# A transformer block with 4-bit feed-forward weights: the first half's chain first, the second half's attention among the feed-forward units

## The chip, the cores and the metric

The kernel runs on one core of a Trainium2 chip. The metric is the device time of one execution in microseconds, the median of the runs. PE is the matrix engine, DVE the vector engine, ACT the scalar engine, POOL the GpSimd engine; SP issues most of the loads.

## The reference, cut to what matters

The input x has 1024 tokens of 256 features. Six vectors of modulation come from one small product. In short:

```python
sa, ca, ga, sb, cb, gb = six 256-wide parts of silu(c) @ wmod
ga, gb = sign * maximum(abs, 0.25)
h = layernorm(x) * (1 + ca) + sa
c = h @ W_to_kv.T @ W_compress.T              # 32 features
ch = layernorm(c) * gamma + beta
q, k, v = ch @ W_q.T, ch @ W_k.T, ch @ W_v.T   # rope on q and k
o = softmax(causal(q @ k.T / sqrt(32))) @ v
z = o @ W_comp2lat.T
x = x + ga * (z @ W_to_kv + z @ W_out_res.T + b_out_res)
h = layernorm(x) * (1 + cb) + sb
gate, up = h @ Wg.T, h @ Wu.T                  # 2048 features, 4-bit weights with scales
x = x + gb * ((gelu_tanh(gate) * up) @ Wd.T)
```

## The kernel before, in words

Each engine has one list of instructions in program order, and the lists meet only in semaphores; the order written in the code is the order in which an engine runs.

The 1024 tokens are two halves of 512 (`h` 0 and 1), each of four tiles of 128. Attention is causal, so the first half has 4 key blocks and the second 8 (`blocks(h)`). Products that need accuracy are made of three matmuls on a high and a low part: ACT writes the high part (a rounded copy) and DVE or POOL the low part (value minus high part). So the probabilities exist as PH (ACT, a second exp) and PL (`probs_low`), the hidden state as H with `h_hi` and `h_lo`, the weights as WS with `split_gu`/`split_d` (ACT) and `low_gu`/`low_d` (POOL), the product of gate and up as IS with `inter_hi` (ACT) and `inter_low` (POOL, later DVE).

The feed-forward has 8 groups of 256 features. A unit is one half of a group for one half of the tokens: 16 units (0 to 15) for the first half of tokens, then 16 for the second. For unit n PE does `gate_up(n)`, 12 matmuls of 512 columns, and two units later `down(n)`, 12 matmuls of 256 columns. In between ACT does `gelu(n)`, DVE `inter_full(n)` (gelu times up), ACT `inter_hi(n)`, POOL `inter_low(n)`. `gate_up(n+1)` waits for `gelu(n)` and `inter_full(n)`, since one pair of PSUM banks serves all units except unit 1, which has banks of its own.

The weights of group G serve units 2G and 2G+1. They come as 4-bit codes: ACT takes the bytes (`take_bytes`), DVE decodes in five steps (`decode`, lines 692 to 704), ACT splits (`split_gu`, line 398, which waits for the decoded group), POOL makes the low part. Groups 0 and 1 are decoded by hand-placed calls, the others by `decode_more` after each `inter_full`, with six steps done before unit 0 (`STEPS_AT_START`).

The order now: both halves go through the norm, the latent projection and q, k, v in an interleaved way, then the second half's scores, row maxima and its exps of blocks 0 to 6 are done before `gate_up(0)`; the rest of its attention lies between units 0, 1 and 2, and `output(1)` behind `gate_up(2)`. The residual and the statistics of the second half are done by DVE after units 1 to 3.

`stay_warm` issues matmuls on a tile of zeros. The table of functions of ACT is loaded ahead of the first exp and ahead of the first gelu. All copies, casts and scalings on ACT go with either.

Of the kernel before, what the change touches and what calls it, by code (L numbers as in the profile page):

```python
# [67 lines left out]
STEPS_AT_START = 6  # L68
H0_BLOCK = 4
# [3 lines left out]
def build_block(nc, x, wmod, c_col, attn64, attn32, b_out, consts, rope, packed, scales, out):  # L73
    with ExitStack() as ctx:  # L74
# [10 lines left out]
        MODA_B, GA_B, WC_B, WO_B = 4, 5, 6, 7  # L85
# [7 lines left out]
        bout_sb = sb("bout_sb", [P, D])  # L93
# [13 lines left out]
        gab = sb("gab", [P, D])  # L107
        gb_b = sb("gb_b", [P, D])
        wsum = sb("wsum", [DLAT, D])
# [46 lines left out]
        x_in = [sem("x_in0"), sem("x_in1")]  # L156
        c_in, a64_in, a32_in, cst_in, bout_in, rope_in = sem("c_in"), sem("a64_in"), sem("a32_in"), sem("cst_in"), sem("bout_in"), sem("rope_in")
# [8 lines left out]
        wsum_ready = sem("wsum_ready")  # L166
# [4 lines left out]
        moda_done = sem("moda_done")  # L171
# [8 lines left out]
        gab_ready = sem("gab_ready")  # L180
# [20 lines left out]
        xres_ready = sem("xres_ready")  # L201
# [83 lines left out]
        def unit_banks(n):  # L285

            return (Y, Y + 1) if isinstance(n, int) and n == 1 else (GATE, UP)
# [5 lines left out]
        def _(sp):  # L293
            sp.dma_start(xres[:, 0:HT, :], x_d[:, 0:HT, :]).then_inc(x_in[0], 16)
            sp.dma_start(cst[:], consts).then_inc(cst_in, 16)
            sp.dma_start(wmod_sb[:, :, 0:2 * D], wmod_d[:, :, 0:2 * D]).then_inc(wmod_in[0], 16)
            sp.dma_start(xres[:, HT:, :], x_d[:, HT:, :]).then_inc(x_in[1], 16)
            sp.dma_start(wmod_sb[:, :, 2 * D:], wmod_d[:, :, 2 * D:]).then_inc(wmod_in[1], 16)
            sp.dma_start(rope_sb[:], rope).then_inc(rope_in, 16)
# [13 lines left out]
        def _(act):  # L313
            act.dma_start(c_sb[:], c_col).then_inc(c_in, 16)
            act.dma_start(a64[:], attn64).then_inc(a64_in, 16)
            act.dma_start(a32[:], attn32).then_inc(a32_in, 16)
            act.dma_start(bout_sb[:], b_out.unsqueeze(0).to_broadcast([P, D])).then_inc(bout_in, 16)
# [5 lines left out]
            def norm1_out(h):  # L323
                act.wait_ge(t1_done, h + 1)
                if h == 1:
                    act.wait_ge(c_done, 1)
                for k in range(KT) if h else (0,):
                    act.activation(xnT[:, k, :], bank(4 * h + k), ACT.Copy).then_inc(t1_ready, 1)

# [34 lines left out]
            def stage_h0():  # L364
# [3 lines left out]
                for e in range(2):  # L368
                    if e == 1:
                        act.wait_ge(h_full, 1)  # L370
                    act.activation(H[:, 0, 0, e, :], bank(e), ACT.Identity, bias=mods[:, M_SB + e:M_SB + e + 1],
                                   scale=mods[:, M_CB + e:M_CB + e + 1]).then_inc(h_hi, 1)

# [45 lines left out]
            norm1_out(0)  # L419
            take_bytes(0)  # L420
# [53 lines left out]
        def _(pool):  # L474
# [16 lines left out]
            def add_bias(h):  # L491

                pool.wait_ge(gab_ready, 1)
                pool.wait_ge(x1n_ready, HT * (h + 1))
# [702 lines left out]
```

## Time and profile before

| | us |
|---|---|
| median of 3 runs | 225.3 (224.9 to 228.08) |
| the profiled execution | 225.71 |
| its span, first to last instruction | 223.9 |
| PE busy | 201.6 (90%) |
| DVE busy | 138.9 (62%) |
| ACT busy | 90.6 (40%) |
| POOL busy | 105.2 (47%) |
| mean granted clock of PE | 0.942 of full |

Busy matmul time is not the same as matmul work: matmuls overlap in the pipeline, and 46 of them (15.5 us) work on the tile of zeros. A group of instructions is named by its line, engine, operation and tiles; L865 is the line of the helper that issues all matmuls, so these are told apart by tiles and shape.

### The profile page before, as it was taken

How to read it: one execution, taken by the hardware profiler on the slowest of the kernel's cores; microseconds unless marked ns; L12 is line 12 of the kernel's file. 1: busy time of each engine (PE TensorE's matmuls, PEld its weight loads, DVE VectorE, ACT ScalarE, POOL GpSimd, SP SyncE). 2: the span in 40 equal slices, each digit the busy share in tenths (PEclk: the TensorE clock that was granted, in tenths of full speed). 3: DMA queues.
4: the chain of work that ended last, by engine and by line, in shares of the span. 5: the costliest groups of instructions: out<-in, count | busy, mean ns of one | idle time of the engine just before them, and what ended most of it. 6: DMA issues, size and time to landing. Idle time of an engine off the chain costs nothing. (4 is left out here: it accounts for less than half of the span.)

```text
span 223.9 us, 3085 instructions
## 1 busy us (share of the span) xinstructions
PE 201.6 (90%) x1064; PEld 161.6 (72%) x1064; DVE 138.9 (62%) x249; ACT 90.6 (40%) x151; POOL 105.2 (47%) x78
## 2 busy tenths in 40 slices
PE   7998998799867984989999999997989999999991
PEld 2494596584545872868888988886778888888891
DVE  1656864938979789999999512575953333333234
ACT  2001321434176842544364356542343543543320
POOL 4412314506050666496996994660606515515200
PEclk9976975579999999999999999999999999999997
DMA  6999775400000000000000000000020000000002
GB/s 190 329 315 203 181 220 190 162 18 3 0 0 1 0 0 3 1 0 0 1 3 0 0 3 0 0 0 3 0 95 0 0 0 0 3 0 0 0 1 94
DMA packets 5645, 11.31 MB, mean 50 GB/s; under 512 B 544, under 2 KB 2752, under 8 KB 5632
## 3 DMA queue, kind: packets, MB, share of 16 engines
q1 hardware_dynamic: 5216, 10.82, 16.6%
q10 hardware_dynamic: 416, 0.33, 0.5%
q8 instruction: 7, 0.11, 0.2%
q14 instruction: 6, 0.05, 0.1%
HBM read 10.09 MB, written 1.05 MB: 50 GB/s over the span
## 5 line engine op out<-in xcount | busy, mean ns | idle before, releaser
L865 PE MATMUL ps<-H,WS 128*128 128x512 f32 x384 | 95.4, 395 | 8.6 <-DVE wmod_sb L721 5.7
L865 PEld LDWEIGHTS ps<-H,WS 128*128 128x128 f32 x384 | 69.6, 188 | 24.8 <-DVE wmod_sb L721 7.8
L865 PEld LDWEIGHTS ps<-WS,IS 128*128 128x128 f32 x384 | 49.8, 191 | 3.2 <-issue 1.1
L865 PE MATMUL ps<-WS,IS 128*128 128x256 f32 x384 | 51.0, 283 | 0.5 <-DVE wmod_sb L721 0.3
L417 ACT ACTIVATE IS<-wmod_sb 128x512 fp32r<-128x512 f32 x32 | 20.2, 632 | 69.4 <-PE ps L865 39.7
L514 POOL TENSOR_TENSOR WS<-wbuf,WS 128x1024 fp32r<-128x1024 f32 x16 | 39.1, 2441 | 9.8 <-ACT WS L398 9.8
L721 DVE TENSOR_TENSOR wmod_sb<-ps,wmod_sb 128x512 f32<-128x512 f32 x32 | 22.0, 688 | 31.8 <-PE ps L865 25.7
L519 POOL TENSOR_TENSOR WS<-wbuf,WS 128x512 fp32r<-128x512 f32 x16 | 22.4, 1402 | 39.8 <-ACT WS L405 39.8
L282 DVE TENSOR_TENSOR IS<-wmod_sb,IS 128x512 fp32r<-128x512 f32 x18 | 12.8, 710 | 24.4 <-ACT IS L417 23.6
L282 POOL TENSOR_TENSOR IS<-wmod_sb,IS 128x512 fp32r<-128x512 f32 x14 | 21.3, 1529 | 13.7 <-ACT IS L417 11.0
L411 ACT ACTIVATE wmod_sb<-ps 128x512 f32<-128x512 f32 x32 | 18.7, 584 | 5.8 <-PE ps L865 5.8
L489 POOL TENSOR_TENSOR rstd<-var,power 128x4 f32<-128x4 f32 x6 | 7.7, 1279 | 21.5 <-DVE var L564 11.8
L398 ACT ACTIVATE WS<-wbuf 128x1024 fp32r<-128x1024 f32 (+1 forms) x16 | 16.8, 1049 | 0.0
L865 PE MATMUL ps<-idle 128*128 128x512 bf16 x46 | 15.5, 484 | 1.3 <-POOL idle L475 1.3
L865 PE MATMUL ps<-PH,VS 128*128 128x512 f32 (+3 forms) x24 | 9.7, 435 | 3.4 <-DVE PL L256 2.8
L703 DVE SCALAR_TENSOR_TENSOR wbuf<-nib,wbuf 128x768 f32<-128x768 fp8e3 x8 | 12.5, 1562 | 0.0
L865 PEld LDWEIGHTS ps<-idle 128*128 128x128 bf16 x46 | 5.1, 120 | 8.5 <-issue 5.5
L389 ACT ACTIVATE nib<-wbuf 128x768 uint8<-128x768 uint8 x8 | 6.7, 840 | 8.7 <-DMA wbuf<-scales 8.7
L700 DVE SCALAR_TENSOR_TENSOR wbuf<-nib,wbuf 128x768 f32<-128x768 fp8e3 x8 | 10.0, 1255 | 0.0
L405 ACT ACTIVATE WS<-wbuf 128x512 fp32r<-128x512 f32 (+1 forms) x16 | 9.9, 617 | 0.0
L497 POOL TENSOR_TENSOR xres<-xres,gab 128x256 f32<-128x256 f32 x8 | 6.8, 874 | 6.6 <-DVE gab L784 6.6
L697 DVE SCALAR_TENSOR_TENSOR nib<-nib,mag 128x384 uint32<-128x384 uint32 x8 | 9.5, 1187 | 0.2
(116 smaller groups left out, 209.3 us busy)
## 6 DMA issues: line engine op xcount, KB each, us to landing
wbuf<-packed SPq DMA_DIRECT2D x8, 384.0 KB
wbuf<-scales SPq DMA_DIRECT2D x8, 384.0 KB
xres<-x SPq DMA_DIRECT2D x2, 512.0 KB, 6.2
wmod_sb<-wmod SPq DMA_DIRECT2D x1, 1024.0 KB, 10.4
out<-xres SPq DMA_DIRECT2D x4, 256.0 KB, 2.2
wmod_sb<-wmod SPq DMA_DIRECT2D x1, 512.0 KB, 7.3
rope_sb<-rope SPq DMA_DIRECT2D x1, 512.0 KB, 10.9
cst<-consts SPq DMA_DIRECT2D x1, 322.0 KB, 5.0
```

The costliest lines, as they stand in the source:

```text
L282: engine.tensor_tensor(IS[:, b, 1, :], inter[:, b, :], IS[:, b, 0, :].bitcast(F32), ALU.subtract).then_inc(i_lo, 1)
L398: act.activation(WS[:, par, 0, :, 0:2, :], src[:, :, 0:2, :], ACT.Copy).then_inc(wgu_hi, 1)
L405: act.activation(WS[:, par, 0, :, 2, :], src[:, :, 2, :], ACT.Copy).then_inc(wd_hi, 1)
L411: act.activation(gel[:, b, :], bank(unit_banks(n)[0]), ACT.Gelu_apprx_tanh).then_inc(gelu_done, 1)
L417: act.activation(IS[:, b, 0, :], inter[:, b, :], ACT.Copy).then_inc(i_hi, 1)
L514: pool.tensor_tensor(WS[:, par, 1, :, 0:2, :], wgroup(g)[:, :, 0:2, :], WS[:, par, 0, :, 0:2, :].bitcast(F32), ALU.subtract).then_inc(wgu_ ...
L519: pool.tensor_tensor(WS[:, par, 1, :, 2, :], wgroup(g)[:, :, 2, :], WS[:, par, 0, :, 2, :].bitcast(F32), ALU.subtract).then_inc(wd_lo, 1)
L697: dve.scalar_tensor_tensor(codes, codes, 0x80808080, mag[:], ALU.bitwise_and, ALU.bitwise_or).then_inc(chain, 1)
L700: dve.scalar_tensor_tensor(wbuf[:, g, 0, :], vals[:, 1, :], FP8E3_BIAS, wbuf[:, g, 1, :], ALU.mult, ALU.mult).then_inc(chain, 1)
L703: dve.scalar_tensor_tensor(wbuf[:, g, 1, :], vals[:, 0, :], FP8E3_BIAS, wbuf[:, g, 1, :], ALU.mult, ALU.mult).then_inc(dec_done, 1)
L721: dve.tensor_tensor(inter[:, b, :], bank(unit_banks(n)[1]), gel[:, b, :], ALU.mult).then_inc(inter_done, 1)
L865: return pe.matmul(o, lhsT, rhs, start=start, stop=stop)
```

## The change

- The first norm is split: DVE only subtracts the mean (`center1`), and the reciprocal deviation is applied in `compress`, once the projection is done. The columns of `ca` are made ahead of those of `sa`.
- The bias of the output projection is a third matmul into `wo` instead of a DVE product and eight POOL additions (`add_bias` goes). x is loaded in three pieces, the constants in two.
- The modulation columns of the second norm and the gate `gb` are made ahead of `project_qkv(0)`; `gb` is copied by ACT (`gate_out`) at once.
- PE does the second half's projection tile by tile between steps of the first half's attention. Of the `stay_warm` matmuls 18 are left of 46.
- All of `decode(0)` stands ahead of the first `probs_low`. `compress(1)` stands ahead of `out_stack(0)`. `residual1` takes the four reciprocals in one instruction and does the statistics tile by tile. `gamma_beta` of the second half and the full copy of the first half's hidden state move from DVE to ACT.
- The second half's scores are done in two pieces, four ahead of `gate_up(0)` and four between `gate_up(0)` and `gate_up(1)`; its row maxima on DVE stand ahead of `inter_full(0)`.
- All key scores, exps, low parts and products with v of the second half stand among units 2 to 6, `output(1)` behind `gate_up(7)`, `residual1(1)` behind `inter_full(8)`.
- Unit 0 has the banks of its own instead of unit 1. `decode(1)` stands behind `inter_full(0)`; the other groups' steps follow with no steps ahead of unit 0; `split_gu(G)` moves from ahead of `gelu(2G-2)` to ahead of `gelu(2G-1)`.

The core of the diff (input handling, semaphores and banks are left out):

```diff
+            def gate_out():
+
+                act.wait_ge(gb_done, 1)
+                act.activation(gb_b[:], bank(GB_B, D), ACT.Copy).then_inc(gb_out, 1)
...
             out_high(0)
+            gamma_beta1()
+            split_gu(0, 0)
             v_high(1)
-            take_bytes(2)
-            split_gu(0, 0)
             split_d(0, 0)
             qk_high(1)
-            act.wait_ge(gb_done, 1)
-            act.activation(gb_b[:], bank(3, D), ACT.Copy).then_inc(gb_out, 1)
-            max_rows(1)
-            exps(1, 0, H0_BLOCK)
             stage_h0()
-            exps(1, H0_BLOCK, 2 * HT - 1)
-            take_bytes(3)
-            split_gu(1, 1)
-            exps(1, 2 * HT - 1, 2 * HT)
-            split_d(1, 1)
 
             for n in range(UNITS + 2):
-                G = n // 2 + 1
-                if n % 2 == 0 and G > 1:
-                    if G + 2 < GROUPS:
-                        take_bytes(G + 2)
+                G = (n + 1) // 2
+                if n % 2 == 0 and n // 2 + 2 < GROUPS:
+                    take_bytes(n // 2 + 2)
+                if n % 2:
                     split_gu(G, G % GROUPS)
                 gelu(n, n % 2, n >= 2)
-                if n == 0:
+                inter_hi(n, n % 2, n >= 2)
+                if n % 2:
+                    split_d(G, G % GROUPS)
+                if n == 2:
+                    max_rows(1)
+                    exps(1, 0, 2)
+                elif n == 3:
+                    exps(1, 2, 4)
+                elif n == 4:
+                    exps(1, 4, 6)
+                elif n == 5:
+                    exps(1, 6, 8)
+                elif n == 6:
                     out_high(1)
-                inter_hi(n, n % 2, n >= 2)
-                if n % 2 and G > 1:
-                    split_d(G, G % GROUPS)
...
             low_gu(0, 0, 0)
             low_d(0, 0, 0)
             rsqrt(N_LN2)
-            for b in range(1, 2 * HT, 2):
-                probs_low(pool, 1, b, b + 1)
-            low_gu(1, 1, 1)
-            low_d(1, 1, 1)
             for n in range(POOL_UNITS):
-                G = n // 2 + 1
-                if n % 2 == 0 and G > 1:
+                G = (n + 1) // 2
+                if n % 2:
                     low_gu(G, G % 2, G)
+                if n == 3:
+                    probs_low(pool, 1, 1, 2)
+                elif n == 5:
+                    probs_low(pool, 1, 5, 6)
                 inter_low(pool, n, n % 2, n >= 2)
-                if n % 2 and G > 1:
+                if n == 3:
+                    probs_low(pool, 1, 3, 4)
+                elif n == 5:
+                    probs_low(pool, 1, 7, 8)
+                if n % 2:
                     low_d(G, G % 2, G)
...
             def steps_before(n):
 
-                return STEPS_AT_START + 5 * n // 2
+                return 5 * max(0, n - 1) // 2
...
+            decode(0)
+            probs_low(dve, 0, 0, HT)
             compress(1)
+            out_stack(0)
             normc(1)
+            residual1(0)
             rotate(1)
             split_v(1)
+            norm2(0, range(HT))
             split_qk(1)
+            row_max(1, 0, 4)
             h_low(0, (0, 1))
+            row_max(1, 4, len(pieces(1)))
 
             for n in range(UNITS + 2):
                 inter_full(n, n % 2, n >= 2)
...
+                if n == 0:
+                    decode(1)
                 elif n == 3:
+                    probs_low(dve, 1, 0, 1)
+                    probs_low(dve, 1, 2, 3)
+                elif n == 4:
+                    probs_low(dve, 1, 4, 5)
+                elif n == 5:
+                    probs_low(dve, 1, 6, 7)
+                elif n == 7:
+                    out_stack(1)
+                elif n == 8:
+                    residual1(1)
...
                 decode_more(steps_before(n), steps_before(n + 1))
...
             stack_qk(1)
+            transpose2(0)
+            scores(1, 0, 4)
+            gate_up(0, 0, 0, 0, 0, first=True, later=False)
+            scores(1, 4, len(pieces(1)))
+            pe.wait_ge(h_full, 2)
             gate_up(1, 0, 0, 0, 1, later=False)
 
             for n in range(2, UNITS + 3):
...
                 if n == 2:
+                    max_rows(1)
+                elif n == 3:
+                    attend(1, 0, HT)
+                    key_scores(1, 3, HT + 3)
+                elif n == 4:
+                    attend(1, 2, HT + 2)
+                    key_scores(1, 5, HT + 5)
+                elif n == 5:
+                    attend(1, 4, HT + 4)
+                    key_scores(1, 7, HT + 7)
+                elif n == 6:
+                    attend(1, 6, HT + 6)
+                elif n == 7:
                     output(1)
...
                 down(d, d // 2, d // UNITS, d // 2 % 2, d % 2, first=d % UNITS == 0, last=d == UNITS - 1)
+                if n == 2:
+                    for b in range(3):
+                        key_scores(1, b, HT + b)
+                elif n == 3:
+                    attend(1, 1, HT + 1)
+                    key_scores(1, 4, HT + 4)
+                elif n == 4:
+                    attend(1, 3, HT + 3)
+                    key_scores(1, 6, HT + 6)
+                elif n == 5:
+                    attend(1, 5, HT + 5)
+                elif n == 6:
+                    attend(1, 7, HT + 7)
```

## Rows read from the trace of the kernel before

**Rows 1.** Busy time of each engine by stretch, granted clock, DMA.
```profile
core 0: us, PE busy (x) PEld busy (x) DVE busy (x) ACT busy (x) POOL busy (x), PEclk, DMA share, GB/s
28.24:48.59 20.35, 18.44 (x81) 14.82 (x81) 11.96 (x26) 5.10 (x12) 6.36 (x7) 0.58 0.48 160
...
79.22:137.56 58.34, 53.26 (x300) 45.62 (x301) 47.22 (x60) 27.50 (x44) 45.31 (x26) 1.00 0.00 1
137.56:218.58 81.02, 78.56 (x454) 68.56 (x453) 34.98 (x50) 35.21 (x56) 32.09 (x18) 1.00 0.02 7
```

**Rows 2.** PE in order of time, one unit: start, length, operation.
```profile
119.92 2.91 PE L865 MATMUL ps<-H,WS 128*128 128x512 f32 x12
122.67 1.59 PE L865 MATMUL ps<-WS,IS 128*128 128x256 f32 x12
124.10 2.91 PE L865 MATMUL ps<-H,WS 128*128 128x512 f32 x12
```

**Rows 3.** PE in order of time, between the first scores and `max_rows(0)`.
```profile
29.39 2.60 PE L865 MATMUL ps<-silu,wmod_sb 128*128 128x1 f32 x16
31.86 3.60 PE L865 MATMUL ps<-wcm,xnT 128*128 128x32 f32 x16
35.39 1.92 PE L865 MATMUL ps<-cst,nmax 128*32 128x128 f32 x8
```

**Rows 4.** DVE in order of time, three decode steps that ran undisturbed.
```profile
73.80 0.56 DVE L697 SCALAR_TENSOR_TENSOR nib<-nib,mag 128x384 uint32<-128x384 uint32 x1
...
103.79 0.94 DVE L700 SCALAR_TENSOR_TENSOR wbuf<-nib,wbuf 128x768 f32<-128x768 fp8e3 x1
104.66 0.95 DVE L703 SCALAR_TENSOR_TENSOR wbuf<-nib,wbuf 128x768 f32<-128x768 fp8e3 x1
```

**Rows 5.** DVE in order of time, three steps of the first half's chain.
```profile
40.55 1.21 DVE L256 TENSOR_TENSOR PL<-PF,PH 128x512 fp32r<-128x512 f32 x1
...
47.84 0.75 DVE L650 SCALAR_TENSOR_TENSOR OS<-o_hi,cst,ps 128x512 fp32r<-128x512 f32 x1 [2.75 <-ACT o_hi L362]
...
63.37 2.35 DVE L586 TENSOR_SCALAR xn<-xres,mv,rstd 128x256 f32<-128x256 f32 x4
```

**Rows 6.** DVE groups by shape: count, busy us, mean ns, idle before.
```profile
L721 DVE TENSOR_TENSOR wmod_sb<-ps,wmod_sb 128x512 f32<-128x512 f32 x32 | 22.0, 688 | 31.8 <-PE ps L865 25.7 <-issue 4.5 <-ACT wmod_sb L411 1.5
...
L659 DVE SCALAR_TENSOR_TENSOR xres<-ps,rden,xres 128x256 f32<-128x256 f32 x8 | 3.9, 484 | 0.3
...
L641 DVE TENSOR_REDUCE nmax_p<-ps 128x1 f32<-128x512 f32 x5 | 3.3, 680 | 0.0
```

**Rows 7.** POOL groups by shape.
```profile
L514 POOL TENSOR_TENSOR WS<-wbuf,WS 128x1024 fp32r<-128x1024 f32 x16 | 39.1, 2441 | 9.8 <-ACT WS L398 9.8
...
L282 POOL TENSOR_TENSOR IS<-wmod_sb,IS 128x512 fp32r<-128x512 f32 x14 | 21.3, 1529 | 13.7 <-ACT IS L417 11.0 <-DVE wmod_sb L721 2.6
L489 POOL TENSOR_TENSOR rstd<-var,power 128x4 f32<-128x4 f32 x6 | 7.7, 1279 | 21.5 <-DVE var L564 11.8 <-DVE var L598 9.7
```

**Rows 8.** ACT groups by shape.
```profile
L411 ACT ACTIVATE wmod_sb<-ps 128x512 f32<-128x512 f32 x32 | 18.7, 584 | 5.8 <-PE ps L865 5.8
L398 ACT ACTIVATE WS<-wbuf 128x1024 fp32r<-128x1024 f32 x10 | 10.5, 1051 | 0.0
...
L355 ACT ACTIVATE PF<-ps 128x512 f32<-128x512 f32 x6 | 3.6, 602 | 1.8 <-PE ps L865 1.8
```

**Rows 9.** All engines in order of time around a decode step at 85 us.
```profile
85.21 2.74 POOL L514 TENSOR_TENSOR WS<-wbuf,WS 128x1024 fp32r<-128x1024 f32 x1 [0.31 <-ACT WS L398]
85.64 3.12 DVE L703 SCALAR_TENSOR_TENSOR wbuf<-nib,wbuf 128x768 f32<-128x768 fp8e3 x1
...
89.82 0.50 PE L865 MATMUL ps<-H,WS 128*128 128x512 f32 x1 [2.49 <-DVE wmod_sb L721]
```

**Rows 10.** ACT in order of time around its load of the function table.
```profile
75.29 0.63 ACT L405 ACTIVATE WS<-wbuf 128x512 fp32r<-128x512 f32 x1
75.94 1.28 ACT L411 ACT_TABLE_LOAD   x1
77.24 0.60 ACT L411 ACTIVATE wmod_sb<-ps 128x512 f32<-128x512 f32 x1
```

More of the change, by code:

```diff
@@ L67, with build_block @@
 POOL_UNITS = 2 * (GROUPS - 1)
-STEPS_AT_START = 6
-H0_BLOCK = 4
 H1_UNIT = 12
-def build_block(nc, x, wmod, c_col, attn64, attn32, b_out, consts, rope, packed, scales, out):
+def build_block(nc, x, wmod, c_col, attn64, attn32, b_row, consts, rope, packed, scales, out):
     with ExitStack() as ctx:
@@ L368, in stage_h0 @@
                 for e in range(2):
-                    if e == 1:
-                        act.wait_ge(h_full, 1)
                     act.activation(H[:, 0, 0, e, :], bank(e), ACT.Identity, bias=mods[:, M_SB + e:M_SB + e + 1],
                                    scale=mods[:, M_CB + e:M_CB + e + 1]).then_inc(h_hi, 1)
+                act.wait_ge(c_done, 2)
+                for e in range(2):
+                    act.activation(hfull[:, e, :], bank(e), ACT.Identity, bias=mods[:, M_SB + e:M_SB + e + 1],
+                                   scale=mods[:, M_CB + e:M_CB + e + 1]).then_inc(h_full, 1)
             def stage_h1(e):
@@ L419, in _ @@
             norm1_out(0)
+            gate_out()
             take_bytes(0)
@@ L552, in link, with tile_stats, layer_var @@
                 dve.wait_ge(chain, steps[0])
-            def layer_stats(h, k):
+            def tile_stats(i):
+                dve.bn_stats(stats[:, i, :], xres[:, i, :]).then_inc(chain, 1)
+                steps[0] += 1
+            def layer_var(h, k):
                 tiles = range(HT * h, HT * (h + 1))
-                for i in tiles:
-                    dve.bn_stats(stats[:, i, :], xres[:, i, :]).then_inc(chain, 1)
-                    steps[0] += 1
                 dve.wait_ge(chain, steps[0])
@@ L593, in compress @@
                 dve.wait_ge(c_done, h + 1)
-                link(dve.tensor_tensor(cc[:, h], bank(4 * h + 2, HT * DC).rearrange("p (j d) -> p j d", j=HT),
-                                       cbias[:].unsqueeze(1).to_broadcast([P, HT, DC]), ALU.add))
+                dve.wait_ge(rstd_ready[N_LN1 + h], 1)
+                for j in range(HT):
+                    dve.scalar_tensor_tensor(cc[:, h, j, :], ps[:, 4 * h + 2, DC * j:DC * (j + 1)],
+                                             rstd[:, N_LN1 + h, j:j + 1], cbias[:], ALU.mult, ALU.add).then_inc(chain, 1)
+                    steps[0] += 1
+                dve.wait_ge(chain, steps[0])
                 link(dve.tensor_tensor(csq[:, h], cc[:, h], cc[:, h], ALU.mult))
@@ L1010, in transpose2, with gate_up @@
                     for k in range(KT):
-                        last = pe.transpose(ps[:, 4 * h + k, P * j:P * (j + 1)], xn[:, h, j, P * k:P * (k + 1)], ident)
+                        last = pe.transpose(ps[:, 4 * h + k, P * j:P * (j + 1)], xn[:, h, j, k:D:KT], ident)
                 last.then_inc(t2_done, 1)
-            def gate_up(n, G, h, par, e, first=False, later=True, after_own_banks=False):
+            def gate_up(n, G, h, par, e, first=False, later=True):
                 banks = unit_banks(n)
@@ L1087, in _ @@
             attend(0, 3, 3)
+            project_c(1, (3,))
+            stay_warm(4, 2)
+            output(0)
+            stay_warm(4, 2)
+            transpose_c(1)
             project_qkv(1)
-            output(0)
-            stay_warm(6, 3)
+            stay_warm(6, 4)
             stack_qk(1)
-            stay_warm(4, 10)
-            scores(1, 0, len(pieces(1)))
-            pe.wait_ge(x1_ready, HT)
-            products(bank(3, D), [(silu[:, k:k + 1].to_broadcast([P, P]), wmod_sb[:, k, GB * D:(GB + 1) * D])
-                                  for k in range(KT)]).then_inc(gb_done, 1)
-            max_rows(1)
-            stay_warm(4, 4)
-            for b, k in blocks(1):
-                key_scores(1, b, k)
-                if b == 2 * HT - 2:
-                    gate_up(0, 0, 0, 0, 0, first=True, later=False)
-                if b >= 2:
-                    attend(1, b - 2, k - 2)
-                if b == H0_BLOCK - 1:
-                    transpose2(0)
-            pe.wait_ge(gb_out, 1)
+            transpose2(0)
[3 more added lines that the diff above has]
+            pe.wait_ge(h_full, 2)
             gate_up(1, 0, 0, 0, 1, later=False)
-            attend(1, b - 1, k - 1)
-            attend(1, b, k)
             for n in range(2, UNITS + 3):
-                gate_up(n, n // 2, n // UNITS, n // 2 % 2, n % 2, first=n == UNITS, after_own_banks=n == 2)
+                gate_up(n, n // 2, n // UNITS, n // 2 % 2, n % 2, first=n == UNITS)
                 if n == 2:
+                    max_rows(1)
[11 more added lines that the diff above has]
+                elif n == 7:
                     output(1)
```

262 lines of the change are left out of this document (115 added, 147 removed).

## The prediction

> **What bounds the kernel now.** I read the busy times by stretch first [rows 1]. The reader should see four stages. Until 70.72 us a latency chain runs (norm, latent projection, rope, scores, softmax of the first half, then scores of the second); PE's granted clock is 0.58 from 28.24 to 48.59, so its small matmuls cost about double there. From 137.56 to 218.58 the feed-forward runs with PE busy 78.56 of 81.02 us: nothing but fewer PE microseconds would shorten it. From 218.58 to the end, 5.32 us, lie the last scaling and stores. Between, from the third unit's gate matmuls (79.22) to the fifteenth's (137.56), PE is busy 53.26 of 58.34 us and DVE 47.22. One undisturbed unit takes 4.18 us [rows 2], so twelve take 50.2.
>
> The change rearranges everything ahead of the fifteenth unit and nothing behind it. So the prediction is one number: when unit 14 (counted from 0) starts, against 137.56. The sum is made against the profiled execution, 225.71 us (span 223.9); the median of the runs is 225.3, so 0.4 comes off at the end.
>
> **Part 1: the road to the first units.** Taken away from the first half's chain: the POOL power ahead of the first norm, 16 tiny matmuls of 2.60 us and the second half's projection of 3.60 us, both of which stand between the first scores and `max_rows(0)` at 35.39 [rows 3]. Only one tile of that projection (a quarter, 0.9) stays there. But the chain is also given work earlier: the tiny matmuls and the 256-wide products of the second gate now stand on PE ahead of `project_qkv(0)`, and no warming matmuls lie between, so I keep PE at the low clock's prices. I put the first scores at 30.0 (now 28.24; estimated 29.1 to 31.9), and `max_rows(0)` at 32.2 to 34.1 (now ends 37.31).
>
> DVE then has the two casts for the output weight (about 1.05) and all five decode steps of group 0 in front of the first low part of the probabilities. Three of the steps run 0.56, 0.94 and 0.95 us undisturbed [rows 4]; with the two short ones this is 3.1 to 3.7. So the first low part starts near 36.8, now 40.55 [rows 5]. Attention of the half ends about 41.3. `compress(1)` is now queued on DVE ahead of `out_stack(0)`, and waits for the projection tile that PE does behind the last `attend`; that puts the stack at 43.8 to 44.6, now 47.84 to 48.59 [rows 5]. Gain so far: 4.
>
> Residual and statistics of the half (four of 0.48 [rows 6], four statistics, aggregation) end near 49.8. Here a queue takes part back: on POOL `low_gu(0)`, `low_d(0)` and only then the power of the second norm are in line, 2.44, about 1.3 and 1.0 to 1.3 us [rows 7], and `low_gu(0)` waits for `split_gu(0)` (1.05 [rows 8]), which ACT issues after `gamma_beta1`. I put that split at 47.4 to 48.5, the power at 53.3, `norm2` at 53.4 (now 63.37 [rows 5]). Gain now 10.
>
> Then: transposes 55.3; four ACT passes to H and the full copy, 58.3; DVE splits q and k, takes four row maxima (2.05), the two low parts (1.3), 60.1; unit 0's third group of matmuls waits for that, so unit 0 ends at 62.0. Four more maxima, 0.68 for a full one [rows 6], end at 65.1, and these stand in front of `inter_full(0)` on DVE (0.69 [rows 6]). This is the cost of the scores in front: unit 0's product at 65.9 instead of about 63. Behind it comes `decode(1)`, 3.6, at 69.5; `split_gu(1)` 1.05, `low_gu(1)` 2.44 [rows 7, 8]; **unit 2 starts at 73.1**, now 79.22. Bounds: 71 (full clock in the chain, decode undisturbed) and 76 (low clock everywhere, each long decode step stretched). Gain 6.1 (3.2 to 8.2).
>
> **Part 2: units 2 to 13.** Two things in the new order cost time here.
>
> First, decode has no lead. Now group G is decoded some three units before ACT splits it. After, the last three steps of group G run behind `inter_full(2G-2)`, ACT's next instruction is `split_gu(G)`, which waits for them, and behind it in ACT's queue stands `gelu(2G-1)`. From the end of unit 2G-2's up matmuls: 0.69, decode 0.56 + 0.94 + 0.95, split 1.05, low part 2.44, and 0.4 for semaphores [rows 4, 6, 7, 8] make 7.0 to unit 2G. PE has 5.6 of its own in between (two downs of 1.43 and one gate_up of 2.75 [rows 2]). A step that meets a POOL operation costs more: 3.12 instead of 0.95 while POOL ran 2.74, and PE waited 2.49 for it [rows 9]. POOL's `inter_low` (1.53) [rows 7] falls right on these steps, so 1.1 more is likely in some pairs.
>
> Second, the exps of the second half move in between the gelus. One table load is in the middle of this kernel, 1.28 us, where the function goes from exp to gelu [rows 10]. After, ACT goes exp, gelu, exp, gelu from unit 2 to unit 6: eight more loads, 10.3 us of ACT. ACT's queue in those units: take the bytes or split, gelu 0.58, cast, load, two exp pairs of about 1.0 [rows 8], load. The Trainium skill's "ScalarE: Activation LUTs", under "What ACT_TABLE_LOAD costs", puts 1.38 us of drain beside the load, 2.66 a switch, and asks for all calls of one set before the next. The trace shows the load alone: the split ends at 75.92, the load runs 75.94 to 77.22, gelu starts at 77.24 [rows 10]. By the page, five switches on the path would add 6.9 and give 251; I go by the row.
>
> The walk, in us after unit 2's start. Unit 2's product at 3.6; max rows done at 4.8; exps of blocks 0 and 1 with the load end at 8.1. `split_gu(2)` 9.15, load and gelu(3) 11.0, `inter_full(3)` 11.75, and only behind it DVE's low part of block 0, 12.6. PE, which finished unit 3's up at 8.75, **waits 4** there. Unit 4 starts at 16.2. `split_d(2)` waits for `down(1)` at 15.3, load, exps to 19.2, bytes, load, gelu(4) 21.9, product 22.7, load, block 4's exps 25.7, its low part 26.4, and decode of group 3 only then, 28.9. Split 30.0, load, gelu(5) 31.9; POOL's low part of the weights 32.5 and of block 5, 33.5: PE **waits 4.8** and unit 6 starts at 34.1. Unit 7 starts at 39.2. Decode of group 4, split, gelu(7), product and `out_stack(1)` end at 46.4, PE **waits 4.4** before the output matmuls; unit 8 at 48.6. `residual1(1)` with its statistics (about 4.5 us of DVE) stands in front of the decode of group 5: unit 10 waits **5.6** and starts at 62.7. Then two pairs with the bare decode chain and norm2: unit 12 at 74.5, unit 14 at 85.0. PE's own work in this stretch is 50.2 + 1.0 (max rows) + 1.6 (key scores) + 4.2 (attend) + 0.9 (output) + 0.8 (transposes) = 58.7, so the walk has 26 of waits.
>
> I charged three collisions of 1.1. Of the eight last decode steps in the trace four run at about 0.95, like the one of [rows 4], so I take half of that off and a little for loads that start under a wait: **83**. Bounds: 76 (no collision, loads partly under waits) and 90 (collisions of 2 us in each pair).
>
> **Sum.** 73.1 + 83 = 156.1 against 137.56: 18.5 later; 225.7 + 18.5 - 0.4 = **244 us**. Its own range: 71 + 76 = 147 gives 235, 76 + 90 = 166 gives 254.
>
> Edits that I cost at nothing: the split of the first x load and the order of the loads (the bytes are the same), the bias row as a matmul (it stands in front of the transposes and could wait up to a microsecond for its load, inside the bounds of part 1), `gate_out` on ACT, the last group's steps.
>
> **Rivals.** (a) PE stays the bound: ACT and DVE keep ahead, and the extra attention matmuls fill PE's wait for decode. The place is unit 4: it must start at about 11 after unit 2, not 16. Then units 2 to 13 take 58.7 and 73.1 + 58.7 = 131.8, 5.8 earlier: **219.5**, faster by 2.6%. For it: in units 2 to 6 PE has 1.4 to 2 us of attention beside the 5.6, about the decode chain's excess. Against: the loads and the order of the queues are fixed in the code, and the sum for unit 3 needs no collision to be late. Chance 0.08.
> (b) Gelu's table serves exp as well, and the eight loads are not there; no row here has an exp behind a gelu, so the trace can't say. Five lie on the path, 6.4: **237**. Chance 0.10.
> (c) The same, and both parts at their low ends: 71 + 76 - 6.4 = 140.6, 3 later, **229**. Chance 0.10, and three quarters of this within 2%.
> (d) The road doesn't get shorter: the low clock and the bias load hold the first half back, unit 2 starts at 79 as now: **250**. Chance 0.12.
> Forecast 0.60.
>
> **How the numbers follow.** 2% (4.5 us, 220.8 to 229.8) is about what a measurement of this kernel tells from no change. Faster 0.08 by (a). Within: three quarters of (c) and a little of the lower tail, 0.09. Slower: the rest, 0.83. The range from 229 to 254 leaves out (a), the lower part of (c), and the forecast's and (d)'s upper tails, 0.2 in all.
>
> **What would show it.** In the changed profile: unit 2's gate matmuls at 71 to 76; ten table loads in all on ACT, 1.28 each, between units 2 and 7; PE idle 4 to 5 us ahead of the first matmuls of `attend(1,0)` and `attend(1,5)`, of `output(1)` and of unit 10, released by the low parts, OS and WS; ACT's split waiting on the last decode step. Behind unit 14 the trace should be as it is now. Unit 4 less than 12 behind unit 2 would make me wrong first; so would a gelu that follows an exp with no load.

## The result, and the profile after

The changed kernel takes **258.27 us** (median of 4 runs, 256.98 to 261.02) beside 225.1 for the kernel before in the same job: ratio 1.142, 95% interval [1.131, 1.153]. The forecast was 244 with a range to 254. The direction is right; the loss is 33 us where 18.5 were worked out.

The profiled execution took 259.29 us, its span 257.5. A profile is of one execution, and those of edits 4, 6 and 9 below are of one that took 1.5 to 1.8% more than the fastest of its kernel. The busy times of the changed kernel by stretch, cut at the starts of units 0, 2, 8 and 14:

```profile
core 0: us, PE busy (x) PEld busy (x) DVE busy (x) ACT busy (x) POOL busy (x), PEclk, DMA share, GB/s
30.00:62.81 32.81, 26.81 (x108) 17.92 (x106) 21.99 (x51) 12.13 (x24) 5.55 (x4) 0.69 0.25 81
62.81:78.52 15.71, 7.19 (x32) 5.02 (x31) 11.43 (x19) 7.29 (x11) 3.93 (x3) 0.90 0.00 1
78.52:132.32 53.80, 39.96 (x192) 32.28 (x193) 18.53 (x28) 31.15 (x45) 23.26 (x16) 0.90 0.00 0
132.32:171.91 39.59, 30.48 (x154) 25.93 (x153) 24.53 (x38) 15.56 (x25) 20.24 (x14) 0.87 0.01 1
171.91:253.00 81.09, 79.15 (x456) 69.28 (x456) 33.92 (x53) 34.07 (x54) 32.62 (x18) 1.00 0.02 7
```

From unit 14 on it is the kernel before [rows 1]: 85.6 us to the end of the span, 86.3 before. Unit 2 starts at 78.52 (79.22 before, 73.1 forecast) and the twelve units after it take 93.4 us (58.3 before, 83 forecast). In these 93.39 us PE is busy 39.96 + 30.48 = 70.4 and idle 22.95. The walk had 58.7 of work and 26 of waits. So the waits came out a little smaller than forecast; **the matmuls took 11.7 us longer than they were priced**, and the granted clock beside them is 0.90 and 0.87, where [rows 1] have 1.00.

PE of the changed kernel in order of time, the largest waits (idle before and its releaser in brackets):

```profile
33.80 0.33 PE L856 MATMUL ps<-KS,QS 96*128 96x128 f32 x1 [1.75 <-DVE KS L635]
...
78.52 4.76 PE L856 MATMUL ps<-H,WS 128*128 128x512 f32 x12 [7.15 <-POOL WS L516]
95.88 0.67 PE L856 MATMUL ps<-PH,VS 128*128 128x512 f32 x1 [4.87 <-DVE PL L253]
118.84 0.42 PE L856 MATMUL ps<-PH,VS 128*128 128x384 f32 x1 [4.25 <-POOL PL L253]
130.31 0.74 PE L856 MATMUL ps<-WOS,OS 128*128 128x258 f32 x4 [1.47 <-DVE OS L653]
145.74 5.25 PE L856 MATMUL ps<-H,WS 128*128 128x512 f32 x12 [4.90 <-POOL WS L516]
159.42 4.25 PE L856 MATMUL ps<-H,WS 128*128 128x512 f32 x12 [2.83 <-POOL WS L516]
171.91 2.99 PE L856 MATMUL ps<-H,WS 128*128 128x512 f32 x12 [1.38 <-issue]
```

The reader should see two things in one row: the wait, and the length of what follows. Twelve gate matmuls take 2.91 in [rows 2]; behind a long wait they take 4.76, 5.25, 4.25. The windows on these places show why:

```profile
78.52:80.50 1.98, 1.98 (x5) 1.59 (x6) 1.34 (x2) 0.66 (x1) 1.98 (x2) 0.50 0.00 0
80.50:83.20 2.70, 2.70 (x9) 1.88 (x7) 0.00 (x0) 0.60 (x1) 0.54 (x1) 0.66 0.00 0
83.20:84.20 1.00, 1.00 (x9) 0.79 (x9) 0.88 (x2) 0.00 (x0) 0.00 (x0) 1.00 0.00 0
...
95.99:99.40 3.41, 3.41 (x13) 3.03 (x14) 0.00 (x0) 0.00 (x0) 0.00 (x0) 0.50 0.00 0
119.90:123.30 3.40, 3.40 (x9) 2.64 (x8) 1.09 (x3) 3.37 (x7) 1.87 (x3) 0.50 0.00 0
...
145.74:148.50 2.76, 2.76 (x7) 2.18 (x8) 1.36 (x2) 0.66 (x1) 2.76 (x3) 0.50 0.00 0
...
160.86:164.25 3.39, 3.39 (x11) 2.66 (x10) 2.09 (x3) 0.60 (x1) 1.07 (x1) 0.50 0.00 0
```

PE stood still for 7.15 us and comes back at the lower of its two levels (0.50, 1.2 GHz): 5 gate matmuls in 1.98 us at 78.52, where [rows 2] have 12 in 2.91. At 83.20 the clock is at 1.00 again. The other four long waits are followed by 0.50 too.

ACT of the changed kernel, the exps between the gelus of units 2 and 3:

```profile
87.25 1.28 ACT L367 ACT_TABLE_LOAD   x1
88.54 0.60 ACT L367 ACTIVATE PF<-ps 128x512 f32<-128x512 f32 x1
...
90.47 1.08 ACT L412 ACTIVATE WS<-wbuf 128x1024 fp32r<-128x1024 f32 x1
91.56 1.28 ACT L425 ACT_TABLE_LOAD   x1
92.86 0.60 ACT L425 ACTIVATE wmod_sb<-ps 128x512 f32<-128x512 f32 x1
```

Ten loads of 1.28 us in all (one stands ahead of the first exp), as forecast, with nothing beside the load: the split ends at 91.55, gelu starts at 92.86. The drain that the Trainium skill's "ScalarE: Activation LUTs", "What ACT_TABLE_LOAD costs", puts beside it isn't in these rows.

### The profile page after: what moved, and what is told of

Same layout as the page of the kernel before. It is cut to its first block and busy times, and to the rows that moved or that the text cites. A ratio compares the mean times of both kernels' runs of the same rounds, so it can differ in the third digit from the quotient of the medians.

```text
span 257.5 us, 3039 instructions
## 1 busy us (share of the span) xinstructions
PE 212.3 (82%) x1040; PEld 172.0 (67%) x1040; DVE 125.8 (49%) x245; ACT 103.9 (40%) x162; POOL 91.8 (36%) x69
## 5 line engine op out<-in xcount | busy, mean ns | idle before, releaser
L856 PE MATMUL ps<-H,WS 128*128 128x512 f32 x384 | 101.5, 416 | 19.4 <-POOL WS L516 15.4
L856 PEld LDWEIGHTS ps<-H,WS 128*128 128x128 f32 x384 | 74.7, 201 | 36.6 <-issue 18.3
L431 ACT ACTIVATE IS<-wmod_sb 128x512 fp32r<-128x512 f32 x32 | 20.2, 632 | 73.7 <-PE ps L856 60.3
L279 POOL TENSOR_TENSOR IS<-wmod_sb,IS 128x512 fp32r<-128x512 f32 x14 | 19.8, 1417 | 44.0 <-ACT IS L431 43.9
L425 ACT ACTIVATE wmod_sb<-ps 128x512 f32<-128x512 f32 x32 | 18.8, 588 | 12.3 <-PE ps L856 12.2
L504 POOL TENSOR_TENSOR rstd<-var,power 128x4 f32<-128x4 f32 x6 | 6.1, 1016 | 40.4 <-DVE var L603 28.0
L856 PEld LDWEIGHTS ps<-PH,VS 128*128 128x128 f32 x24 | 5.4, 229 | 12.8 <-issue 9.7
L253 DVE TENSOR_TENSOR PL<-PF,PH 128x512 fp32r<-128x512 f32 (+3 forms) x8 | 5.4, 669 | 17.0 <-ACT PH L368 8.9
L699 DVE SCALAR_TENSOR_TENSOR wbuf<-nib,wbuf 128x768 f32<-128x768 fp8e3 x8 | 8.6, 1076 | 0.3
L702 DVE SCALAR_TENSOR_TENSOR wbuf<-nib,wbuf 128x768 f32<-128x768 fp8e3 x8 | 8.7, 1090 | 0.0
L856 PE MATMUL ps<-idle 128*128 128x512 bf16 x18 | 7.2, 549 | 1.3 <-POOL idle L490 1.3
L856 PE MATMUL ps<-wcm,xnT 128*128 128x32 f32 x32 | 7.5, 383 | 0.0
L856 PEld LDWEIGHTS ps<-wcm,xnT 128*128 128x128 f32 x32 | 7.1, 315 | 0.4 <-issue 0.4
```

The costliest lines, as they stand in the source:

```text
L279: engine.tensor_tensor(IS[:, b, 1, :], inter[:, b, :], IS[:, b, 0, :].bitcast(F32), ALU.subtract).then_inc(i_lo, 1)
L425: act.activation(gel[:, b, :], bank(unit_banks(n)[0]), ACT.Gelu_apprx_tanh).then_inc(gelu_done, 1)
L431: act.activation(IS[:, b, 0, :], inter[:, b, :], ACT.Copy).then_inc(i_hi, 1)
L504: pool.tensor_tensor(rstd[:, k, :], var[:, k, :], power[:], ALU.pow).then_inc(rstd_ready[k], 1)
L699: dve.scalar_tensor_tensor(wbuf[:, g, 0, :], vals[:, 1, :], FP8E3_BIAS, wbuf[:, g, 1, :], ALU.mult, ALU.mult).then_inc(chain, 1)
L702: dve.scalar_tensor_tensor(wbuf[:, g, 1, :], vals[:, 0, :], FP8E3_BIAS, wbuf[:, g, 1, :], ALU.mult, ALU.mult).then_inc(dec_done, 1)
```

## The experiments

My theory after the result: the mechanisms of the forecast are there at about their size, and the missing 15.8 us at unit 14 (171.91 for 156.1) come from PE's clock, which falls in the waits and also at the start. The rivals: table loads that cost more than I charged, the decode without lead, the residual ahead of the decode, and steps of the road that have nothing to do with the clock. All kernels are the changed kernel with the edit named; in brackets behind a ratio to the kernel before is the 95% interval. "The loop" is the time from unit 2 to unit 14 in the profile.

**1. Matmuls on the tile of zeros in four waits.** Each stands behind a wait that ends early in the gap, so that it delays nothing.

```diff
             for n in range(2, UNITS + 3):
+                if n == 2:
+                    pe.wait_ge(nm_ready, 1)
+                    stay_warm(4, 26)
+                elif n in (10, 12):
+                    pe.wait_ge(x1_ready, 2 * HT)
+                    stay_warm(6, {10: 18, 12: 10}[n])
                 gate_up(n, n // 2, n // UNITS, ...)
...
                 elif n == 3:
+                    pe.wait_ge(m_ready, 2)
+                    stay_warm(7, 18)
                     attend(1, 0, HT)
```

> The changed kernel with matmuls on the tile of zeros put into four of PE's waits: ahead of unit 2, of the first product with v of the second half (unit 3), of units 10 and 12; nothing is left out. Theory of the clock: each wait of 5 us or more lets the granted clock fall to half, so that the work behind it runs at half pace; kept warm, unit 2 and unit 10 take 2.8 instead of 4.7 and 5.1 us, unit 12 2.8 instead of 4.1, and the time falls by about 7 us, to 251. Rival, that the slow matmuls lie in time that would be waited anyway: the units are shorter and the waits longer by as much, time 258 as before.

254.51 us, 1.138 [1.126, 1.149]; the time lies between the theory's 251 and the rival's 258. PE in order of time:

```profile
78.69 3.00 PE L856 MATMUL ps<-H,WS 128*128 128x512 f32 x12 [1.53 <-issue]
...
116.35 4.49 PE L856 MATMUL ps<-H,WS 128*128 128x512 f32 x12
...
142.68 2.99 PE L856 MATMUL ps<-H,WS 128*128 128x512 f32 x12 [1.02 <-issue]
...
154.12 3.01 PE L856 MATMUL ps<-H,WS 128*128 128x512 f32 x12 [0.67 <-issue]
```

The warmed units take 3.0. Unit 6, whose wait (ahead of `attend(1,5)`) got none, still takes 4.49. The loop falls from 93.4 to 86.4 with every dependency where it was. The profiled execution took 252.47, 6.8 less than that of the changed kernel, and both have their first scores late (33.95 and 33.80), so these two are alike up to unit 2. The median falls by only 3.8, and the intervals of the two ratios overlap; the pair that settles it in time is edits 9 and 10.

**2. The exps of the second half as scaled copies**, so that ACT needs no further table; this leaves the probabilities out.

```diff
+                    func = ACT.Copy if h else ACT.Exp
-                    act.activation(PF[...], src, ACT.Exp, scale=SCALE)
+                    act.activation(PF[...], src, func, scale=SCALE)
```

> The changed kernel with both exps of the second half replaced by scaled copies of the same shapes (the probabilities of the second half are so left out of the computation); ACT then needs no table of exp between the gelus. Theory of the prediction: eight loads go, five of them on the path, so 6.4 us and up to 3 more where a wait gets too short for the clock to fall: 249 to 252. Rival, that the loads lie under other waits: 257 or more.

252.46 us, 1.123 [1.109, 1.136], but the loop only falls from 93.4 to 90.7 (units 2 to 8: 51.1 for 53.8). The rest of its profile's gain is that unit 2 starts at 73.70, on a road on which nothing was changed; more on that below.

**3. Decode with a lead**: `decode(1)` ahead of the last four row maxima, the other groups' steps one unit earlier.

```diff
-                return 5 * max(0, n - 1) // 2
+                return 5 * n // 2
...
             h_low(0, (0, 1))
+            decode(1)
             row_max(1, 4, len(pieces(1)))
...
-                if n == 0:
-                    decode(1)
...
```

> The changed kernel with the decode of group 1 moved ahead of the last four row maxima, into an idle stretch of DVE, and with the steps of the other groups one unit earlier (two steps behind unit 0, group G done behind unit 2G-3). Theory that decode has no lead: unit 2 starts some 4 us sooner, ACT's splits stop waiting for DVE, and the waits ahead of units 10, 12 and 14 go or shrink: 12 to 20 us less, 238 to 246. Rival, that the exps and their loads on ACT set the pace of units 2 to 8 and the residual that of unit 10: only unit 2's gain and the waits ahead of 12 and 14 come back, 8 us, about 250.

249.89 us, 1.108 [1.096, 1.121]; loop 87.5. Units 8 to 12 take 20.2 for 27.1, which is the decode chain of part 2. Units 2 to 8 take 54.9 for 53.8: no gain at all. Unit 2 starts at 73.58, with a wait of 4.54 in front of it in place of 7.15.

**4. `residual1(1)` behind the decode steps** of unit 8, not in front of them.

> The changed kernel with the residual and statistics of the second half behind the three decode steps that follow unit 8's product, and not ahead of them. Theory: the split of group 5 waits 3.7 us less, so the wait ahead of unit 10 (4.9 us) is short enough for the clock to hold, and the time falls by 4 to 6 us, to 252 to 254. Rival, that unit 9's product, now behind the residual on DVE, is late by as much: 258.

254.01 us, 1.129 [1.118, 1.141]. PE, units 10 and 12:

```profile
141.75 2.97 PE L856 MATMUL ps<-H,WS 128*128 128x512 f32 x12 [1.24 <-issue]
...
154.56 5.46 PE L856 MATMUL ps<-H,WS 128*128 128x512 f32 x12 [4.22 <-POOL WS L516]
```

Unit 8 to unit 10 takes 9.8 us, in the changed kernel 13.4. But the wait moves to unit 12 (4.22, then 5.46 at the low clock), and units 10 to 12 take 12.8 (13.7). What DVE does ahead of the next group's last steps is now the second half's norm, which waits for POOL's power (0.73 and no wait in the changed kernel):

```profile
146.87 1.74 DVE L589 TENSOR_SCALAR xn<-xres,mv,rstd 128x256 f32<-128x256 f32 x2 [1.19 <-POOL rstd L504]
```

**5. 14 warming matmuls at the start, not 10.**

> The changed kernel with 14 matmuls on the tile of zeros at the start, as before, and not 10. In the profile of the changed kernel all ten run 0.43 us apart, and the small matmuls of the first 30 us at half pace; where ten were just enough (the profile of e2), unit 0 started near 58 us and not 63. Theory that the four missing ones cost the first half's chain its clock: unit 0 starts at 58, 3 to 5 us less, 253 to 255. Rival, that the clock falls later in the chain anyway: less than 1.5 us, 257.

257.88 us, 1.152 [1.144, 1.161]: nothing. Here my theory that the start alone holds the road back fell; `stack_qk(1)` was still slow (3.30). In its profile unit 2 starts at 75.47, 3 earlier, and the loop takes 94.3.

**6. Edits 2 and 3 together** (this again leaves the probabilities out).

> e2 and e3 together: copies in place of the second half's exps (their probabilities left out) and decode ahead by a unit. Each alone left the stretch from unit 2 to unit 8 nearly as long as it was (51 and 55 us, 54 in the changed kernel). Theory that either of the two alone holds units 2 to 8, so that the other's removal shows nothing: together the stretch falls to 42 or less and the time to 238 or less. Rival, that the stretch is held by the attention among the units itself (low parts behind products in the queues of DVE and POOL, a split that waits for a down): it stays near 50, and the time at 246.

238.52 us, 1.063 [1.054, 1.072]; loop 76.5, units 2 to 8 44.65, a little above the theory's 42. The copies alone gave 2.7 there, the lead alone nothing, both 9.2. That looks as if either one alone held this stretch, but its windows in edits 2, 3 and 6 (length, then PE busy) say something else:

```profile
73.70:124.82 51.12, 41.72 (x192) 34.29 (x193) 20.04 (x28) 20.22 (x37) 23.51 (x16) 0.82 0.00 0
...
73.58:128.52 54.94, 42.78 (x192) 33.84 (x193) 24.39 (x29) 30.59 (x45) 25.22 (x16) 0.84 0.00 1
...
76.99:121.64 44.65, 36.41 (x192) 29.79 (x193) 24.75 (x29) 19.66 (x37) 25.07 (x16) 0.96 0.00 1
```

The changed kernel has 53.80 and 39.96. So PE's waits there are 13.8 us, with the copies 9.4, with the lead 12.2, with both 8.2: they shrink by 4.4, 1.7 and 5.6, nearly the sum of the two. **What doesn't add up is the work**: it takes 1.8 and 2.8 longer when one alone is taken away (clock 0.82 and 0.84), and 3.6 less with both (0.96). The split isn't exact, since a slow matmul under another engine's chain can cost nothing. Edits 7 and 12, which keep two of the waits warm, support it: they differ in this stretch by the copies and six matmuls on zeros, and take 49.4 and 43.05, so the copies are worth 6.4 on top of the lead, 1.6 of it by unit 6's clock (2.92 for 4.50). The copies alone with warm waits were not run.

**7. Edit 5, 16 warming matmuls each ahead of unit 2 and `attend(1,0)`, and edits 3 and 4.** Nothing of the computation is left out.

> The changed kernel with 14 warming matmuls at the start, warming ones in the waits ahead of unit 2 and of the first product with v, the decode lead of e3 and the residual of e4; nothing is left out. If the four costs add up (4, 7, 8 and 4 of 33 us, the clock's part halved as waits get shorter): about 238. If the waits of units 2 to 8 take what the others give back: 243 to 246. Either is slower than the kernel before.

245.25 us, 1.097 [1.089, 1.105]; unit 2 at 71.49, loop 80.6. Units 2 to 8 take 49.4; in edit 1, without the lead, 50.6. The best version that keeps the new order is 9.7% slower than the kernel before.

**8. The new first half alone.** The attention of the second half is put back where the kernel before has it, with six decode steps ahead of unit 0; the power of the second norm goes ahead of the weights' low parts; 14 warming matmuls at the start.

```diff
             transpose2(0)
-            scores(1, 0, 4)
-            gate_up(0, 0, 0, 0, 0, first=True, later=False)
-            scores(1, 4, len(pieces(1)))
+            scores(1, 0, len(pieces(1)))
+            max_rows(1)
+            for b, k in blocks(1):
+                key_scores(1, b, k)
+                if b == 2 * HT - 2:
+                    gate_up(0, 0, 0, 0, 0, first=True, later=False)
+                if b >= 2:
+                    attend(1, b - 2, k - 2)
...
```

> The first half's chain as in the changed kernel (with 14 warming matmuls, and POOL's power of the second norm ahead of the weights' low parts), and the second half's scores, row maxima, exps and products with v where the kernel before has them: all exps ahead of the first gelu, six decode steps ahead of unit 0, output behind unit 2, residual behind units 1 to 3. Theory that the road is shorter and only the attention among the units costs: unit 0 starts at 62 to 66 and not at 70.7, the rest is as before: 217 to 221, faster than the kernel before. Rival, that the road gives nothing: 224 to 227.

231.25 us, 1.032 [1.022, 1.042]: slower than both expectations. DVE, its norm of the first half, and PE, the maxima of the second half and unit 0:

```profile
54.77 2.32 DVE L583 TENSOR_SCALAR xn<-xres,mv,rstd 128x256 f32<-128x256 f32 x4
```
```profile
65.56 1.91 PE L860 MATMUL ps<-cst,nmax 128*32 128x128 f32 x8 [1.88 <-DVE nmax L641]
...
76.98 3.00 PE L860 MATMUL ps<-H,WS 128*128 128x512 f32 x12
```

The first half's norm is 8.6 us earlier than in [rows 5] (54.77 for 63.37), but the second half's maxima come at 65.56, in the kernel before at 59.29, and unit 0 with the attention in front of it at 76.98 for 70.72. Units 2 to 14 take 57.3, before 58.3. So the new order buys the first half's lead with the second half's delay; alone it costs 7 us. Not all of this need be the order: of the 6.3 us by which unit 0 is later, 4.1 are there at the first scores (32.33 for 28.24), and between the second half's scores and unit 0 the granted clock is low, where the kernel before has 1.00 from 55.4 to 70.72:

```profile
64.00:75.00 11.00, 7.56 (x21) 4.92 (x22) 6.00 (x10) 4.81 (x10) 1.98 (x2) 0.54 0.00 0
```

With 22 warming matmuls in place of 46, order and clock are not told apart here.

**9. Warming along the road**: edit 5, and matmuls on zeros ahead of `transpose_c(0)` (4), `project_qkv(0)` (3), `scores(0)` (4) and `stack_qk(1)` (10, not 4).

> The changed kernel with 17 more matmuls on the tile of zeros along the first half's chain: ahead of the transposes of the latent (4), of q, k, v (3), of the first scores (4) and of the second half's stacking of q and k (6 more), and 14 instead of 10 ahead of the modulation. Theory A, the low clock costs the road its forecast gain: stack_qk(1), 3.78 us at a clock of 0.50, comes back to about 2, unit 0 starts 3 to 5 us ahead of 62.8 and the time is 253 to 255. Rival B, the road is set by DVE, ACT and POOL waits between small steps: the first scores and the second norm stay within 1 us of where they are and the time is 256.5 to 258.5.

258.02 us, 1.139 [1.130, 1.148]: nothing in the time. In its profile (259.07) unit 2 starts at 75.98, 2.5 earlier, but takes 5.46, and the loop takes 95.7: the gain is given back behind the wait.

**10. Edits 1 and 9 together.**

> The same, with the warming matmuls in the waits ahead of unit 2 (26), attend(1,0) (18) and units 10 (18) and 12 (10). Theory A, clock on the road and clock behind the waits are separate losses and add up: 254.5 less 3 to 5, 249.5 to 251.5. Rival B, only the waits matter: 253.5 to 255. With A the stretch from unit 2 to unit 14 is about 86.4 as with the waits alone and unit 2 starts near 74; with B it starts near 78.5.

247.99 us, 1.104 [1.096, 1.111]. PE of this kernel:

```profile
9.58 1.84 PE L856 MATMUL ps<-silu,wmod_sb 128*128 128x1 f32 x16
...
30.58 0.33 PE L856 MATMUL ps<-KS,QS 96*128 96x128 f32 x1 [0.88 <-DVE KS L635]
...
74.30 2.96 PE L856 MATMUL ps<-H,WS 128*128 128x512 f32 x12 [1.53 <-issue]
...
160.58 3.00 PE L856 MATMUL ps<-H,WS 128*128 128x512 f32 x12 [1.38 <-issue]
```

First scores at 30.58 (forecast 30.0), unit 2 at 74.30 (73.1), unit 14 at 160.58 (156.1), the loop 86.3. With no edit but matmuls on zeros the kernel comes to 4.0 us above the forecast. Edit 9, from which it differs by the matmuls in the four waits alone, took 258.02 in the same job: 10.0 us, with intervals well apart (1.104 and 1.139).

**11. One part of the change in the kernel before**: the full copy of the first half's hidden state on ACT.

> The kernel before with one part of the change alone: the full copy of the first half's hidden state goes from DVE to ACT, behind ACT's two rounded copies, and the low parts wait for it. Theory A, DVE is the engine that is late between unit 0 and unit 3, and two passes of about 0.7 us less bring unit 2 and the end forward by 0.5 to 2 us: 222.8 to 224.3. Rival B, these passes lie under the wait for the row maxima and ACT's two passes now stand in front of the exps: no change or up to 1 us later, 224.3 to 225.5.

224.59 us, 0.996 [0.992, 1.000]: no difference that can be told. The windows of PE behind its wait of 2.50 us, which answers to the one in [rows 9]:

```profile
88.50:90.00 1.50, 1.48 (x6) 1.26 (x7) 1.43 (x5) 1.12 (x2) 0.74 (x1) 0.94 0.00 0
90.00:92.70 2.70, 2.70 (x13) 2.61 (x13) 2.67 (x6) 0.00 (x0) 0.56 (x1) 0.50 0.01 3
```

The wait ends 1.30 us earlier (88.52 for 89.82), but here the clock falls behind it (0.50), `down` takes 2.76 for 1.60, and the next gate matmuls start at 92.73, in the kernel before at 92.74.

**12. All suspects at once**: edits 2, 3, 4 and 9, and fewer warming matmuls in the waits (16, 10 and 6 ahead of unit 2, `attend(1,0)` and unit 12). It leaves the probabilities out.

> All suspects taken away at once: scaled copies in place of the second half's exps (leaves the probabilities out, so that ACT has no further table loads), decode(1) ahead of the last four row maxima and the other groups' steps earlier, the residual of the second half behind the decode steps, the warming matmuls along the first half's chain, and 16 ahead of unit 2, 10 ahead of attend(1,0), 6 ahead of unit 12. Theory A, decode without lead, the table loads, the residual in front and the low clock are the whole loss of the stretch from unit 2 to unit 14: it falls from 93.4 to 66 to 72 (PE's own work is 58.7), unit 2 starts at 70 to 74, and the time is 225 to 232. Rival B, the gains overlap or another wait is next: the stretch stays at 74 to 77 as with the first two alone, and the time is 235 to 239.

236.29 us, 1.040 [1.020, 1.061], where the kernel before took 226.8 in the same job. The loop is 74.2: rival B. Its window, with all matmuls and with those on zeros alone:

```profile
74.47:148.66 74.19, 65.25 (x360) 53.09 (x361) 48.09 (x64) 34.70 (x62) 46.87 (x30) 1.00 0.00 1
...
74.47:148.66 74.19, 3.80 (x16) 1.40 (x16) 0.00 (x0) 1.00 0.00 1
```

So about 61.4 us are work at the full clock, and 12.7 are gaps. Its rows of the last units, of all engines in order of time:

```profile
138.68 1.94 DVE L700 SCALAR_TENSOR_TENSOR wbuf<-nib,wbuf 128x768 f32<-128x768 fp8e3 x1
...
139.75 2.02 POOL L522 TENSOR_TENSOR WS<-wbuf,WS 128x512 fp32r<-128x512 f32 x1
...
140.54 2.05 DVE L703 SCALAR_TENSOR_TENSOR wbuf<-nib,wbuf 128x768 f32<-128x768 fp8e3 x1
...
148.66 1.94 PE L856 MATMUL ps<-H,WS 128*128 128x512 f32 x4 [2.33 <-POOL WS L517]
```

Two decode steps run beside POOL's work (1.94 and 2.05 for 0.95 [rows 4]), and unit 14 waits 2.33. The place of the residual isn't the cause: edit 3, which leaves it in front, has 1.95, 2.05 and the same 2.33. In units 2 to 8 five waits of 0.8 to 1.6 for QS, the low parts and OS are left, 6.0 in all. I see no single cause behind them; none of them was tested alone.

## Why the prediction was wrong

**Part 1, the road: mis-sized ahead of the first scores.** I put these at 30.0 (29.1 to 31.9); they came at 33.80. From there to unit 2 the sum was 43.1 and 44.7 were measured, so 3.8 of the 5.4 us lie ahead of the first scores. In this profile PE works at the low pace there:

```profile
8.56 1.22 PE L856 MATMUL ps<-brow_sb 1*128 1x256 f32 x2
...
11.46 3.41 PE L856 MATMUL ps<-silu,wmod_sb 128*128 128x1 f32 x16
```

The 16 tiny matmuls take 3.41 us, where edit 10 has 1.84, as the kernel before has them. This isn't so in every execution: profiles of kernels whose road is the changed kernel's have the first scores at 30.19 (edit 2), 33.54 (edit 4) and 33.95 (edit 1). Edit 2's, with unit 2 at 73.70, meets the forecast of 30.0 and 73.1 almost exactly. The granted clock of that window is given as 1.00; there only the durations tell. Gain "10" at `norm2` was 6.0 (57.34 for 63.37), and unit 2 was within 1 us of where it had been: rival (d)'s place, by half of rival (d)'s cause. The low clock was there; for the bias row PE had no wait (8.56). Edit 8, with the attention put back, had no gain from this part either.

**Part 2, the loop: the step that failed.** The walk took PE's work, 58.7 us, at undisturbed prices although it put four waits of 4 to 5.6 us between, and part 1 had itself read a clock of 0.58 off a stretch of small matmuls and short waits [rows 1]. The bound of 90 had collisions in it, but no clock. The runs put in its place: behind each long wait the clock is at 0.50 for a few us, the work takes 70.4, not 58.7, and edit 1 takes 7.0 out of the loop by matmuls on zeros alone; in time, edit 10 is 10.0 below edit 9 by the same matmuls. Not all of the 11.7 is clock: edit 12 needs 61.4 at a clock of 1.00, so about 2.7 were priced too low and about 9 are the clock. The loop is 10.4 longer than the 83 of the forecast, and three terms add up to about that: 7.0 go with edit 1, 1.6 are unit 6, whose wait stayed cold there (4.49 for 2.91), and 2 I had taken off the walk for collisions. The Trainium skill's "TensorE: Matmul & The Clock Gate", "Part 1: The HAM clock gate", says that "the default state is throttled, and activity releases the throttle"; the trace agrees (0.50 at 78.52, 1.00 at 83.20), and that sentence should have been held against the walk's own waits.

**The waits were right, but for two.** Forecast and measured: 4.0 and 4.87 ahead of `attend(1,0)`; 4.8 and 4.25 ahead of `attend(1,5)`; 5.6 and 4.90 ahead of unit 10; 26 and 22.95 in all. Unit 12 has a wait in the walk's dates only (11.8 behind unit 10, of which 8.4 are PE's work): 3.4, and 2.83 measured. Wrong were 4.4 ahead of `output(1)`, where 1.47 came, and none ahead of the key scores, where ACT's pass to QS cost 1.4. With the clock held (edit 10) the walk's 85.0 stands beside 86.3, in part by luck: the work is about 63.3 there, not 58.7, and the gaps 23.0, not 26. Unit 4, at 16.2 in the walk, comes at 19.0 and unit 6 at 38.1 for 34.1; the short wait for `output(1)` gives 2.9 back.

**The decode without lead** was right in units 8 to 12: edit 3 takes 6.9 out. In units 2 to 8 it gave nothing, and 1.1 with two waits warm (edits 1 and 7). **The table loads** were right in number and length. Five on the path, 6.4 us, is what the copies gave on top of the lead with two waits warm (edits 7 and 12), 1.6 of it by the clock. Without that they gave 2.7 alone (edit 2) and 11.0 in the loop on top of the lead (87.5 to 76.5, edit 6), 6.0 of the 11.0 in PE's work: the price that I had left out stands in these numbers too.

**The rivals.** (a) falls: unit 4 starts 22.3 us behind unit 2, not 11. (b) falls with the nine loads after the first. (c) falls with both. (d) is half right, as said. The sum that I gave for (c) comes to 228.3, not 229; nothing hangs on that.

**What stays open.** Edit 10 is 6.5 us below edit 1, but edit 9 isn't below the changed kernel. In the profiles the road's gain is given back behind unit 2's wait where that isn't warmed, and kept where it is; 4.4 of the 6.5 is seen as the earlier unit 2. Why the first matmuls run at the full pace in some executions and not in others wasn't settled. Nor was how much of edit 8's 7 us is the order, and what holds the 12.7 us of gaps in edit 12. Matmuls on zeros in the wait ahead of `attend(1,5)` weren't tried.

## What to carry to other kernels

A wait on the matrix engine can have two prices: its own length, and half the pace of the first work behind it. A walk through a schedule that finds waits of several us must price the work after each at the low clock, or say what keeps the engine busy. An edit that shortens a wait can show little in the time, because the work behind it is still slow: split a stretch into waits and work, and test suspects alone and together, before you call one harmless. And work pulled forward for one half of the data is paid by what it stands in front of; compare the later half's dates before you count the earlier half's gain.

## What the runs showed of the hardware that I had not expected

A wait of about 2.5 us can go either way. In the kernel before, PE waits 2.49 [rows 9] and the clock stays at 1.00; in edit 11 the same wait of 2.50 is followed by 0.50 and costs 1.2 us more, which is the whole of the 1.30 that the edit had won. Gains of a microsecond in a stretch with gaps can so vanish without any dependency taking them. In edit 3 a wait of 2.33 ahead of unit 14 is followed by 0.51 (4.57 for the twelve gate matmuls), one of 1.78 ahead of unit 12 by 1.00 (3.02).

A tiny operation on DVE can take as long as POOL's large one: in the changed kernel a 128x4 scaling, 0.17 us in other places, ran from 52.87 beside POOL's 2.35:

```profile
52.76 2.35 POOL L516 TENSOR_TENSOR WS<-wbuf,WS 128x1024 fp32r<-128x1024 f32 x1 [4.31 <-ACT WS L412]
52.87 2.27 DVE L571 TENSOR_SCALAR var<-mv 128x4 f32<-128x4 f32 x1
```

The second norm's power doesn't wait for it, since that stands on POOL behind the weights' low parts until 56.30. What it delays is the rope product behind it on DVE (55.05), for which PE waits 1.09 ahead of `stack_qk(1)`.
